# Cross attentions with few sums of probabilities, their reciprocals spread by transfers, and maxima in three bf16 parts

## The reference, cut to what matters

```
x = x + tanh(g_xattn[0]) * _L0_xattn_ref(_layernorm(x), ctx, mask, ...)   # with rotary positions
x = x + tanh(g_ffn[0])   * _L0_ffn_ref(_layernorm(x), ...)                # light local + heavy routed attention
x = x + tanh(g_xattn[1]) * _L1_xattn_ref(_layernorm(x), ctx, ctx, ...)
x = x + tanh(g_ffn[1])   * _L1_ffn_ref(_layernorm(x), ...)
...
x = x + tanh(g_xattn[3]) * _L3_xattn_ref(_layernorm(x), ctx, ctx, ...)
x = x + tanh(g_ffn[3])   * _L3_ffn_ref(_layernorm(x), ...)                # 8 experts, 2 per token

# each of the three attentions:
scores = einsum('bhqd,bhkd->bhqk', q, k) * scale      # 8 x 16 x 512 x 64
attn   = softmax(scores, axis=-1)
out    = einsum('bhqk,bhkd->bhqd', attn, v) @ Wo + bo
```

## Time and profile before

| | |
|---|---|
| runs | 2517.16, 2515.82, 2509.72 us |
| the profiled execution | 2514.42 us, its span 2512.5 us |
| TensorE busy | 2342.6 us, 93% of the span |
| VectorE (DVE) busy | 1409.9 us, 56% |
| ScalarE (ACT) busy | 961.1 us, 38% |
| mean granted TensorE clock | 0.973 |

### The profile page before, as it was taken

One profiled execution on the slowest core, in us unless ns is written; L12 is line 12 of the kernel. 1 busy time (PEld: TensorE's weight loads), 2 busy tenths in 40 slices (PEclk: granted clock), 3 DMA queues, 4 the chain that ended last, 5 costly groups with the idle time before them and its releaser, 6 DMA issues.

```text
span 2512.5 us, 40654 instructions
## 1 busy us (share of the span) xinstructions
PE 2342.6 (93%) x15494; PEld 1659.9 (66%) x15494; DVE 1409.9 (56%) x2881; ACT 961.1 (38%) x2302; POOL 615.4 (24%) x548
## 2 busy tenths in 40 slices
PE   6997999999999998998999999988984999999998
PEld 4444676776666665444666765544543999999997
DVE  7886654774444455887466533348884444444442
ACT  2366555444554553332233322124643222222222
POOL 3233222252001002211233200024455122222222
PEclk9999999999999999999999999989996999999999
DMA  5012101121001000100001039502126222222221
GB/s 200 1 35 71 60 9 44 34 85 51 26 26 51 26 26 26 70 1 17 1 1 36 1 98 324 179 0 109 44 73 238 64 35 35 35 35 37 36 37 26
DMA packets 73767, 144.70 MB, mean 58 GB/s; under 512 B 11592, under 2 KB 62536, under 8 KB 71120
## 3 DMA queue, kind: packets, MB, share of 16 engines
q1 hardware_dynamic: 41280, 100.94, 11.8%
q0 software_dynamic: 16368, 26.23, 5.3%
q10 hardware_dynamic: 15936, 15.03, 2.1%
HBM read 107.42 MB, written 71.09 MB: 71 GB/s over the span
## 4 chain that ended last, share of the span: by engine, by line
PE 80%; DVE 10%; ACT 4%; issue 2%; POOL 2%; DMA 1%; another core or an unknown queue 0%; SPq 0%; DVEq 0%; POOLq 0%; ACTq 0%
PE PS L2366 14%; PE PS L2392 7%; PE PS L2800 5%; PE PS L1540 4%; PE PS L1531 4%; PE PS L2812 4%; PE PS L2050 3%; PE PS L2062 3%; PE PS L602 3%; PE PS L2869 3%; PE PS L2860 3%; PE PS L2834 3%; DVE mem L1143 2%; PE PS L2905 2%; DVE mem L1148 2%; PE PS L2895 2%
## 5 line engine op out<-in xcount | busy, mean ns | idle before, releaser
L2366 PEld LDWEIGHTS PS<-ctx2T,x_all 128*128 128x128 f32 x3124 | 362.5, 193 | 11.3 <-DVE x_all L2515 6.8
L2366 PE MATMUL PS<-ctx2T,x_all 128*128 128x128 f32 x3124 | 363.1, 276 | 7.2 <-DVE x_all L2515 6.4
L2563 POOL DMA_INDIRECT out_x<-xnT,moe_small x71 | 130.8, 1842 | 430.5 <-ACT xnT L2448 427.8
L2392 PE MATMUL PS<-mem,moe_small 128*128 x852 | 195.7, 379 | 0.8 <-ACT xnT L2448 0.8
L2515 DVE COPY x_all<-mem 128x2816 f32 x71 | 115.5, 1627 | 111.4 <-issue 96.9
L2392 PEld LDWEIGHTS PS<-mem,moe_small 128*128 128x128 f32 x852 | 156.3, 190 | 19.5 <-issue 1.2
L1148 DVE RECIPROCAL mem<-PS 128x512 f32<-128x512 f32 x48 | 160.8, 3350 | 9.7 <-PE PS L671 9.6
L1143 DVE TENSOR_REDUCE mem<-PS 128x32 f32<-128x2048 f32 x48 | 109.8, 2289 | 50.5 <-PE PS L627 49.8
L3185 DVE TENSOR_REDUCE moe_small<-PS 128x2 f32<-128x1024 f32 x64 | 78.4, 1225 | 102.6 <-PE PS L2860 100.3
L3330 POOL TENSOR_TENSOR mem<-mem,moe_small 128x512 f32<-128x512 f32 x64 | 82.3, 1306 | 212.6 <-DVE moe_small L3195 212.6
L2800 PE MATMUL PS<-xnT,mem 128*128 128x512 f32 x256 | 127.6, 621 | 0.8 <-ACT xnT L2984 0.8
(11 more groups left out here) (378 smaller groups left out, 4512.7 us busy)
## 6 DMA issues: line engine op xcount, KB each, us to landing
slots<-in_trash_rows SPq DMA_DIRECT2D x8, 4290.0 KB, 64.4
mem<-in_L_ffn_experts SPq DMA_DIRECT2D x8, 2176.0 KB, 11.5
xn<-unit_rows SPq DMA_DIRECT2D x15, 512.0 KB, 4.2
xn<-slots ACTq DMA_DIRECT2D x53, 130.0 KB, 2.1
x_all<-in_x SPq DMA_DIRECT2D x8, 512.0 KB, 8.4
mem<-unit_rows SPq DMA_DIRECT2D x8, 512.0 KB
out_x<-x_all ACTq DMA_DIRECT2D x8, 512.0 KB, 2.9
unit_rows<-moe_small SPq DMA_DIRECT2D x7, 512.0 KB, 3.2
```

The costliest lines, as they stand in the source:

```text
L2366: last = nc.tensor.matmul(PS[:, moe_bank(j, part), c * P:(c + 1) * P], m.w[:, j % 2, k, at:at + P], m.rowT[:, j % 2, k, :], start=k == 0, ...
L2392: last = nc.tensor.matmul(PS[:, MOE_BANK_Y, 0:D], m.hT[:, j % 2, n, :], w[:, :, at:at + D], start=n == 0, stop=n == KE - 1)
L2563: nc.gpsimd.indirect_dma_start(s.T["out"], bass.IndirectOffsetOnAxis(s.token[:, j % 4:j % 4 + 1], 0), m.result[:, j % 4, :], None, compute ...
```

## The change

**Few sums.** `denominators` uses a second 0/1 table, `sums_of_tile`: the sums of token tile t of a head go to row t of the head's 16 rows, so that 128 x 128 elements hold all of them. For that it runs 16 products of 128 columns instead of 4 of 512. DVE takes the reciprocal of 128 x 128. SP then stores it to a DRAM buffer and, when that has landed, loads it back, each head's 512 values to its 16 partitions. The product on DVE waits for that load. On DVE other work is put between the reciprocal and the product. The last half of a stage goes the old way.

**Maxima in bf16.** The maxima are split in three bf16 parts that add up to them, by four small operations (on GpSimd in L0, on DVE in L1 and L3). The transposes and the product that takes off the maximum run in bf16; the 0/-1 table covers the three parts.

**Order.** In L1 the maxima are turned and copied before the second shifted scores instead of after. In L1 and L3 ACT issues the loads of the next stage in turn 2 or 1, instead of SP. In L0 SP takes the new transfers between its stores. In the light half of the next part, the attention values are put right behind the scores and belong to step j-2 instead of j-1, ACT's copy of them moves likewise, and one load of rows more is issued ahead of the spreading of scores.

```diff
+def split_max(eng, order, s, b):
+    eng.wait_ge(s.sems["max_ready"], 2 * (b + 1))
+    order.mark(eng.tensor_copy(max_part(s, 0), s.max))
+    order.settle()
+    order.mark(eng.tensor_tensor(s.max_rest, s.max, max_part(s, 0), ALU.subtract))
+    order.settle()
+    order.mark(eng.tensor_copy(max_part(s, 1), s.max_rest))
+    order.settle()
+    eng.tensor_tensor(max_part(s, 2), s.max_rest, max_part(s, 1), ALU.subtract).then_inc(s.sems["max_split"], 1)
+
+def spread_recips(sp, s, b, f):
+    k = KD * b + f
+    few = s.recips[f].rearrange("(q r) n -> q r n", r=HD)[:, 0:TB, :].rearrange("q t n -> q (t n)").rearrange("q (o n) -> q o n", o=1)
+    sp.wait_ge(s.sems["recip_ready"], k + 1)
+    sp.dma_start(s.recips[f], s.recip_few).then_inc(s.sems["recip_stored"], 16)
+    sp.wait_ge(s.sems["recip_stored"], 16 * (k + 1))
+    sp.dma_start(s.recip, few.broadcast_to([NH // KD, HD, S])).then_inc(s.sems["recip_spread"], 16)
...
     def turn_max(b):
-        pe.wait_ge(s.sems["max_ready"], 2 * (b + 1))
+        pe.wait_ge(s.sems["max_split"], b + 1)
...
-        for c in range(G):
-            last = nc.tensor.matmul(PS[c * GR:(c + 1) * GR, BANK_DEN, :], s.sums, s.probsT[:, f, c, :], start=True, stop=True)
+            for t in range(TB):
+                for c in range(G):
+                    last = nc.tensor.matmul(PS[c * GR:(c + 1) * GR, BANK_DEN, 0:P], s.sums_of_tile[:, t, :],
+                                            s.probsT[:, f, c, t * P:(t + 1) * P], start=t == 0, stop=t == TB - 1)
...
+        if now and s.max_first:
+            turn_max(n)
         if before:
             scores_of_keys(n - 1, 1, min(2 * n + 2, 2 * B))
...
+        if s.act_loads and n == (1 if handed else 2):
+            act.wait_ge(e.x_updated, s.x_before)
+            for dst, src in s.next.loads:
+                act.dma_start(dst, src).then_inc(s.next.weights_loaded, 16)
...
+    def reciprocals(b, f):
+        dve.wait_ge(s.sems["den_psum"], KD * b + f + 1)
+        if (b, f) == (B - 1, KD - 1):
+            dve.reciprocal(s.recip, PS[:, BANK_DEN, :]).then_inc(s.sems["recip_ready"], 1)
+        else:
+            dve.reciprocal(s.recip_few, PS[:, BANK_DEN, 0:P]).then_inc(s.sems["recip_ready"], 1)
+
     def normalise(b, f):
-        dve.wait_ge(s.sems["den_psum"], KD * b + f + 1)
-        dve.reciprocal(s.recip, PS[:, BANK_DEN, :]).then_inc(s.sems["recip_ready"], 1)
         dve.wait_ge(s.sems["pv_psum"], KD * b + f + 1)
-        dve.wait_ge(s.sems["recip_ready"], KD * b + f + 1)
+        if (b, f) == (B - 1, KD - 1):
+            dve.wait_ge(s.sems["recip_ready"], KD * b + f + 1)
+        else:
+            dve.wait_ge(s.sems["recip_spread"], 16 * (KD * b + f + 1))
...
         if old:
-            normalise(n - 2, 1)
+            reciprocals(n - 2, 1)
         if route:
             norm_scales(n - 3)
         for b in s.stats_in_turn.get(n, ()):
             stats(b)
+        if old:
+            normalise(n - 2, 1)
         if now:
             maxima(n, 1)
+            if not s.split_on_pool:
...
+                split_max(dve, order, s, n)
...
         if before:
-            normalise(n - 1, 0)
+            reciprocals(n - 1, 0)
...
         if n + 2 < B and not m:
             apply(n + 2)
         if route:
             pick_experts(n - 3)
+        if before:
+            normalise(n - 1, 0)
         if old:
             add_out(n - 2)
...
-    for b in range(1, B // 2 + 1):
+    before_scores = SCORE_STEP // CT + 1
+    for b in range(1, before_scores + 1):
         sp.wait_ge(light.sems["xT_psum"], KD * b)
         load_rows(light, b)
...
         light_scores(j)
+        if j >= 2:
+            light_values(j - 2)
         keys(p, nxt)
...
-        if j >= 1:
-            light_values(j - 1)
```

More of the change, by code:

```diff
@@ L53, in shape_constants @@
         out[name] = ((row[:, None] // HD) == half[None, :]).astype(f) * f(scale)
-    out["minus_max"] = np.concatenate([-(row[:, None] == (2 * k + p // SC)[None, :]).astype(f) for k in range(KD)], 1)
+    of_part = (row < 4 * PARTS)[:, None] & (row[:, None] % 4 == (np.arange(KD)[:, None] * 2 + (p // SC)[None, :]).reshape(1, -1))
+    out["minus_max"] = bf16_pairs(-of_part.astype(f))
     out["sums"] = ((p // SC)[:, None] == (np.arange(GR) // HD)[None, :]).astype(f)
+    place = np.arange(GR) % HD
+    of_tile = (place[None, :] == np.arange(TB)[:, None]) | ((place >= TB)[None, :] & (np.arange(TB) == 0)[:, None])
+    out["sums_of_tile"] = (out["sums"][:, None, :] * of_tile[None, :, :]).astype(f).reshape(P, TB * GR)
     swap = np.zeros((P, P), f)
@@ L83 @@
 ROTARY = ("cos_q", "sin_q", "cos_k", "sin_k")
-OF_A_STAGE = ROTARY + ("earlier", "of_head8", "of_head4", "minus_max", "sums")
+OF_A_STAGE = ROTARY + ("earlier", "of_head8", "of_head4", "minus_max", "sums", "sums_of_tile")
 def constant_columns():
@@ L381, in _ @@
                         sp.dma_start(dst, src).then_inc(later.keys_loaded, 16)
-                    for dst, src in later.loads:
+                    for dst, src in later.loads if not s.act_loads else ():
                         sp.dma_start(dst, src).then_inc(later.weights_loaded, 16)
@@ L501, in plan_xattn @@
     s.o = take(2, KD, S)
-    s.recip = take(S)
+    s.recip, s.recip_few = take(S), s.w.take(P)
     s.recip_end = s.a.at
@@ L563, in logits_bank, with max_part, recips_sync @@
     return 2 if b >= B - 2 else BANK_M
+def max_part(s, part):
+    n = 2 * KD * TB
+    return s.max_parts.rearrange("p (g n) -> p g n", g=G)[:, :, part * n:(part + 1) * n]
+def split_max(eng, order, s, b):
[14 more added lines that the diff above has]
+    sp.dma_start(s.recip, few.broadcast_to([NH // KD, HD, S])).then_inc(s.sems["recip_spread"], 16)
+def recips_sync(sp, e, s):
+    for b in range(B):
+        for f in range(KD):
+            if (b, f) != (B - 1, KD - 1):
+                spread_recips(sp, s, b, f)
 def xattn_pe(pe, e, s):
@@ L669, in denominators @@
                 wait_for(pe, m.sems["ranks_ready"], b - 1)
-        for c in range(G):
-            last = nc.tensor.matmul(PS[c * GR:(c + 1) * GR, BANK_DEN, :], s.sums, s.probsT[:, f, c, :], start=True, stop=True)
+        if (b, f) == (B - 1, KD - 1):
+            for c in range(G):
+                last = nc.tensor.matmul(PS[c * GR:(c + 1) * GR, BANK_DEN, :], s.sums, s.probsT[:, f, c, :], start=True, stop=True)
+        else:
+            for t in range(TB):
+                for c in range(G):
+                    last = nc.tensor.matmul(PS[c * GR:(c + 1) * GR, BANK_DEN, 0:P], s.sums_of_tile[:, t, :],
+                                            s.probsT[:, f, c, t * P:(t + 1) * P], start=t == 0, stop=t == TB - 1)
         last.then_inc(s.sems["den_psum"], 1)
@@ L785, in xattn_pe @@
             project_out(n - 2, 0)
-        if now:
+        if now and not s.max_first:
             turn_max(n)
@@ L790, in xattn_pe @@
                 project_out(n - 2, 0)
-            project_out(n - 2, 1)
+            if not s.max_first:
+                project_out(n - 2, 1)
             if now and not s.front:
@@ L837, in units_sync @@
     u = s.units
-    for b in range(EARLY_UNITS):
+    for n in range(1, EARLY_UNITS + 4):
+        if 0 <= n - 2 < B - 1:
+            spread_recips(sp, s, n - 2, 1)
+        if n - 1 < B:
+            spread_recips(sp, s, n - 1, 0)
+        b = n - 4
+        if b < 0:
+            continue
         if b == 3:
@@ L1014, in xattn_act @@
             copy_yT(n - 3)
+        if now and s.max_first:
+            copy_max(n)
         if before:
@@ L2700, in colt_sync @@
         .then_inc(s.sems["scores_spread"], 16)
-    for b in range(B // 2 + 1, B):
+    for b in range(before_scores + 1, B):
         sp.wait_ge(light.sems["xT_psum"], KD * b)
```

71 lines of the change are left out of this document (49 added, 22 removed).

## The result

The changed kernel takes 2606.71 us (median; 2598.79 to 2609.17, 4 runs) against 2516.05 of the kernel before (2509.72 to 2517.16, 4 runs) on the same chip: ratio 1.0365, 95% interval 1.035 to 1.038. It is slower, as forecast, but by 91 us where I had said 20, and outside the range given (2505 to 2572).

What follows compares the result with a forecast made beforehand. It took the loop alternating between nearly full TensorE and DVE as the bound. L0 +6, L1 +8, L3 +5, traffic +2, light half -1 made +20 on 2514.42: 2534.4, as median 2536 us, range 2505 to 2572.

Steps and rivals of the forecast that it cites:

- The load: Second half of the reciprocals' round trip: 256 KB from DRAM back to 128 partitions, taken to land in 2.5 us.
- D: Time from a reciprocal's end to its product's start (store, wait, load, wait): 4.3 us, likeliest 4.0 to 4.6.
- upper end: Highest D kept for the round trip: 5.2 us, with a load of 2.8 and half a microsecond of other traffic.
- 27 per us: Cost in the whole kernel of one microsecond of D: about 8.5 in L0, 10 in L1, 8 in L3.
- The store: First half of the round trip, 64 KB of reciprocals to DRAM: 1.64 us, on a line between 16 and 512 KB.
- 17.84 + D: Steady L0 turn after the change, one round trip counted: 22.1 us against 22.14 before.
- covered trip: L0 turn's other round trip, 8.2 us with maxima and product, beside over 9 of TensorE: hidden up to D = 5.2.
- traffic: ACT's next-stage loads meeting round trips in L3 (+1 to +5) and L1 similarly: 2 us added.
- The sums: Sixteen products of 128 columns on TensorE for the denominators: 1.1 us a call, against 1.09 for the old eight.
- Transfers are slower: Rival: D = 4.75 to 5.2, giving 2548 up to 2560 us, with possible further cost from TensorE stalls; 18%.
- The small products are the cost: Rival: sum products at 68 ns each cost TensorE 50 us, about 15 on the path: 2551 us; 10%.
- hidden and faster: Rival: round trips are hidden and the loop gets shorter; with D = 3.2, 2506 us; 24%.

Runs made afterwards that it cites:

- as changed: The changed kernel itself, run again on another chip as yardstick, against the kernel before: 2597.70 us, ratio 1.0374.
- four copies: Changed kernel with each head's small sums held four times, each 2 KB loaded into 4 partitions instead of 16: 2554.32 us, ratio 1.0201 to the kernel before.
- rows apart: Changed kernel, but each round trip's load reads 128 different rows of an input table; true reciprocals left out: 2548.10 us, one time.
- second halves: Changed kernel with round trips for the second halves (f = 1) alone, first halves as before: 2546.91 us, ratio 1.0174 to the kernel before.
- no round trips: Changed kernel with sums and reciprocals of 512 columns as before and no reciprocal transfers: 2491.56 us, ratio 0.9952 to the kernel before.
- free spreading: Changed kernel without storing and loading reciprocals; the product uses a constant, small sums and reciprocals stay: 2461.61 us, one time.
- experiments 3 and 4: Changed kernel with other load sources: rows apart 2548.10 us, Rows shared 2581.54; then as changed 2597.70 and four copies 2554.32.
- experiment 4: Changed kernel rerun (as changed, 2597.70 us) beside four copies (2554.32 us), with their loads' packets and TensorE's granted clocks compared.
- experiment 2: The run free spreading: changed kernel without stores and loads of reciprocals, product by a constant: 2461.61 us, one time.
- Rows shared: Changed kernel, but each load spreads 8 rows of an input table over 16 partitions each; true reciprocals left out: 2581.54 us, one time.

## Why the prediction was wrong, step by step

**Where the time went, by stage.** From first and last starts of marked lines, one profile each; before is from a slower chip (its median 2516; the kernel before has 2504 to 2506 on the others' chips), and a stage varies by some 3 us between profiles.

| us | before | as changed | four copies | rows apart | second halves | no round trips | free spreading |
|---|---|---|---|---|---|---|---|
| L0 attention | 231.4 | 257.6 | 244.7 | 239.5 | 239.8 | 229.0 | 221.1 |
| light, heavy half | 741.7 | 740.1 | 738.6 | 738.6 | 734.5 | 733.8 | 734.3 |
| L1 attention | 211.5 | 247.4 | 232.7 | 229.8 | 228.0 | 205.0 | 196.7 |
| L2, L3 | 502.8 | 526.0 | 512.4 | 513.8 | 514.9 | 494.3 | 483.8 |

**The load, the step that failed.** I priced it at 2.5 us by a load with 128 rows of 2 KB, "of the same shape". Only its target has the shape. The source is 8 rows taken 16 times each, and that takes 3.8 to 4.4 in most trips (experiments 3 and 4). No row of before has such a source; the one load there that spreads a row, one into 128 partitions, is not slow. Loads from rows apart took 2.6 to 2.8 in most trips, so the price was right for the transfer I had looked at. D came out at 5.5 instead of 4.3, above what I had kept as the upper end. (The terms given for that end, 1.64 + 2.8 + 0.15 + 0.5, add up to 5.1 and not to 5.2.) Between D = 4.3 and 5.5 the loss goes from 42 to 93 us over the kernel before, some 50 of the 71 us that the forecast lacks, 32 of them by my own 27 per us; the other 20 or so are at 4.3 already.

**The store.** 1.64 forecast by a line between two sizes, 1.53 to 1.54 measured. Right.

**The slope, a second fault.** I let one round trip a turn count and hid the other up to D = 5.2. By the L0 chain above a turn goes from 169.42 to 193.73, 24.31 us, of which the two D are 5.96 and 5.50; the rest, 12.85 us, is DVE's own work with its handovers, so DVE's row is 12.85 + 2D; it passes my 17.84 + D at D = 5.0. From there a microsecond of D counts twice a turn. Two other turns of L0, from one small reciprocal to the same of the next turn, bear this out. With rows apart and D of 4.38 and 4.31 a turn takes 22.09 us: my 17.84 + D gives 22.2, DVE's row 21.5. In the changed kernel, with 5.37 and 5.80, it takes 23.98: DVE's row gives 24.0, my sum 23.6 at most. The whole times agree in direction: over the kernel before, about 21 us per us of D between 0.1 and 4.3, 25 from there to 4.6, and 48 between 4.6 and 5.5, a part of this last the clock's (experiment 4). My working of the covered trip compared its 8.2 us with TensorE's 9 and forgot that the second maxima and all that follows on DVE queue behind it.

**What is missing at the D I had forecast.** With D = 4.3 (rows apart) the kernel takes 42 us more than before, not 20. The table gives L0 +8 (forecast +6), L1 +18 (+8), L2 and L3 +11 (+5), the light and heavy half -3 (-1). Most of the rest, as the traces have it, is traffic, which I had put at 2 in all. In L1 the second trip of the changed kernel meets the 4 MB that ACT issues for the next stage:

```profile
1074.84 0.34 SPq L610 DMA_DIRECT2D recips<-mem  x1
1076.41 0.61 SPq L612 DMA_DIRECT2D mem<-recips  x1
...
1089.98 0.69 DVE L1241 TENSOR_TENSOR mem<-PS,mem 128x512 f32<-128x512 f32 x1 [13.29 <-DMA mem<-recips]
```

The load takes 13.6 us instead of 3.9. In L3 the first store meets expert loads:

```profile
1796.19 0.33 SPq L610 DMA_DIRECT2D recips<-mem  x1
1805.08 0.66 SPq L612 DMA_DIRECT2D mem<-recips  x1
```

8.9 us instead of 1.5. The two excesses make 17 us, once each. With rows apart the L1 load takes 8.1 and L3's first store 9.7, so that these two trips have D = 10.7 and 12.5, 14.6 us above twice 4.3; later L3 trips take up to 6.6. That these delays and not something else make up most of the 22 us is read from the traces; a kernel with ACT's loads elsewhere was not run.

**The other terms.** The small reciprocal takes 0.95 us, as worked out, but 45 of the 48 shrink and not 47, since each of the three stages keeps its last half: 108 us of DVE's time and not 113. The four bf16 products take 0.22 to 0.24 in the chains, 0.23 forecast. The sums are 65.5/45 = 1.46 us a call, over the 1.1 taken but under the 2.2 of the rival; with free spreading, at a granted clock of 0.974 over the whole against 0.952, they are 1.18, and harmless by experiment 2. Light half: -1 forecast, 0.11% or 2 to 3 us measured. DVE's busy time fell by 98 for "some 100"; its idle time ahead of the product is 4.6 us a trip, not 2 or 3.

**The rivals.** "Transfers are slower" was the right one, and priced too low: it stopped at D = 5.2 and took most of the path at 27 us per us. It had also named TensorE's clock after stalls, which is seen: 0.96, 0.97 and 0.87 over the attention parts of L0, L1 and L3 before, 0.89, 0.87 and 0.81 now. By the Trainium skill ("DMA: Bandwidth & Descriptors", Anatomy of one DMA), whose fit is for another issuing path, D is an estimated 4.75. That is nearer than my 4.3 and still below the 5.5 measured: the store takes 1.54, under the estimated 2.15 that the fit gives for 64 KB, and the load 3.9, over its 2.6 for 256 KB. "The small products are the cost" is refuted by free spreading, and "hidden and faster" would have needed D well under 4.3.

**Open.** Rows shared and the changed kernel have nearly the same D (most trips 5.3 to 5.6 against 5.3 to 5.9), yet 2581.5 and 2597.7 us. Summed over the 45 trips D is 269 against 277 us, 4 of these 8 in two trips of L0, so about half of the 16 us may be D. The first multiplies by other numbers, and its mean granted clock is 0.955 against 0.950; I have no cause for the rest. And open is what the load would take if its source pattern began with 16 or more while each row is still read 16 times.

## What to carry to other kernels

A transfer is priced by both of its ends: look for a row with the same source pattern, its first dimension too, and where the trace has none, leave the upper end open. A load that keeps the DMA engines half busy and has 8 small packets instead of 16 asks for another order of its source before its bytes are blamed; here 32 rows first instead of 8, each read 4 times instead of 16, took 43 us off the kernel. For a wait put on an engine that works in order, write that engine's whole turn down with every wait in a row and see where it passes the old loop; comparing one trip with its cover misses what queues behind it. Replacing 2.4 us of arithmetic by a round trip through memory pays only below a D that can be worked out (on a straight line between the runs at D = 0.1, -44 us, and 4.3, +42 us, an estimated 2.2, where I had 3.55), and the transfers that other queues have in flight at the time belong in it.

## What the runs showed of the hardware

- Loading 256 KB as 128 rows of 2 KB, from issue to the waiting product: 2.7 us from 128 different rows, 3.0 from 32 rows read 4 times each, 3.9 from 8 rows read 16 times each. SP's issue itself is longer too: 0.33, 0.53 and 0.60 us. A packet of 2 KB takes 84 or 85 ns in all of them; with 8 rows first, 10 or 11 packets are under way at once instead of 18 to 20. What the engines move peaks at 215 GB/s there and at 439 with rows apart.
- One row of 16 KB taken into 128 partitions (2 MB) landed in 6.7 us, 313 GB/s, in the kernel before: reading a row many times need not be slow.
- A row written 1.5 us earlier is read hardly slower than one of an input: 3.98 against 3.88 us.
- A 256 KB load that SP issued amid ACT's 4 MB landed after 13.6 us instead of 3.9, and a 64 KB store amid expert loads after 8.9 instead of 1.5: a small transfer on one queue can be held up by what another queue has in flight.
